# The first recurrence in a new order, with five masked levels of each leaf multiplied by TensorE one by one

## The chip, the cores and the metric

The kernel runs on one core of a Trainium2 chip. The metric is the device time of that core in microseconds (us), as a median of runs; lower is better. All tensors are float32. Five engines work from queues of their own, each strictly in the order in which its instructions were written: TensorE (PE, with its weight loads shown apart as PEld), VectorE (DVE), ScalarE (ACT), GpSimd (POOL) and SyncE (SP, which here only issues DMAs). They meet only at semaphores.

## The reference, cut to what matters

The program is two layers. Each is a modulated layer norm, a linear-attention recurrence with a residual, and a mixture of experts. The change touches the recurrence of the first layer alone (RWKV-6 on x of shape 2 x 1024 x 128, with two heads of 64; the 2 x 1024 tokens are handled as 8 chunks of 128 tokens of both batches).

```python
x_last = jnp.pad(x, ((0, 0), (1, 0), (0, 0)))[:, :t]      # x is the modulated norm
dxa = x_last - x
xm = x + dxa * miu_x
lora_h = jnp.tanh(xm @ A_lora).reshape(b, t, 5, -1)
miu = lambda_ + jnp.einsum('btfi,fic->fbtc', lora_h, B_lora)
xx = x[None] + dxa[None] * miu
w_in, k_in, v_in, r_in, g_in = xx
k = k_in @ Wk.T;  v = v_in @ Wv.T;  r = r_in @ Wr.T
g = jax.nn.silu(g_in @ Wg.T)
w = td_miu + jnp.tanh(w_in @ td_A) @ td_B
decay = jnp.exp(-jnp.exp(w))
# per head and token: S is 64 x 64, u a bonus for the token itself
def step(S, inp):
    ri, ki, vi, di = inp
    kv = ki[:, None] * vi[None, :]
    y = ri @ (S + uh[:, None] * kv)
    return di[:, None] * S + kv, y
# then a norm of y per head (eps 1e-5 * h), times g, times Wo.T, gate and residual
```

## The kernel before, in words

`rwkv_phase` (from L329) takes the 8 chunks one after another. `steps` (L480) writes them out: `front()` prepares chunk 0, then `step(i, q, prepare, tail)` runs for i = 0 to 7, and a last part normalises chunk 7. Buffers of a chunk's inputs have two copies, picked by q. In each call of `step`, every engine does three things mixed in an order fixed by hand:

- **the recurrence of chunk i.** Seven levels (m = 0 to 6) build, by doubling, the decayed r and k in the tiles rl[1..7], kl[1..7] and the products of decays tot[1..7]. At each level DVE multiplies tot and half of rl (L595, L596), POOL multiplies half of kl (L686), and ACT copies the other halves (L765, L767); every engine waits for the others at every level. PE multiplies k and r of a level within leaves of 32 tokens (`leaf_scores`, L855, slots 0 to 4 of the PSUM tile `pair`; slot 0 has the bonus) and, after level 5, the wider blocks (L913, L919). DVE masks the five slots (L613, into prod), adds them up (L616, into leafs) and copies the sum into the diagonal blocks of att (L621). ACT copies the blocks off the diagonal (L784 to L786). PE then multiplies rl[7] by state and att by v (L938, L941), and the transposed kl[7] (ktm, L929 and L776) by v (L946). DVE makes the new state from that (L626, L630).
- **the preparation of chunk i + 1** (prepare): norm (L504, DVE), transpose (L799), modulation (L713, ACT), difference (L641, POOL), lora_input (L510, DVE), two products (L804, L805), tanh (L718, L720, ACT), five small products (L814, L817), mix (L518 on DVE, then L646 on POOL, five instructions on each), and the projections to decay, k, v, r, g (L822 to L838) with their evacuations on ACT (L724 to L742). The last of them (eg, L742) tells that the chunk is ready.
- **the end of chunk i - 1** (tail): the norm of y per head (statistics L535 and L539, deviation L655 and L657 on POOL, normalise L544), transpose, scale, gate (L662), product with Wo (L873), gate and residual (L550, L667), and the input of the expert layer (moe_input, L558 to L572, with L673 and L675 on POOL).

What couples one step to the next is `start`, which DVE, POOL, ACT and PE pass at the head of a step:

```python
if not isinstance(i, int) or i:
    eng.wait_ge(s_state, i * 3)
eng.wait_ge(s_gT, i + 1)
```

So no engine begins the levels of chunk i before the state of chunk i - 1 is written. `keep_busy` (L865) puts 128 x 256 products whose result nobody reads into PE's queue, nine of them in a step with a tail and a preparation. Ahead of the levels, in each step, DVE also makes the four bonus tiles rd and kd (L584 to L587).

Of the kernel before, what the change touches and what calls it, by code (L numbers as in the profile page):

```python
# [22 lines left out]
P = 128  # L23
# [10 lines left out]
LEAF = 32  # L34
# [294 lines left out]
def rwkv_phase(nc, t, const, x_bc, eps_pow, mod_col, mod_row, bank, pair, cst, W0T, s_w0, mv, rstd, W1, s_w1, s_w2, sbw,  # L329
# [8 lines left out]
    with ExitStack() as ctx:  # L338
# [25 lines left out]
        rd = sb("rd", [P, N])  # L364
        kd = sb("kd", [P, N])
        vs = [sb(f"v_sb{q}", [P, BATCH, C]) for q in range(2)]
        eg = sb("eg", [P, N])
        gT = sb("gT", [P, N])
        prod = sb("prod", [P, 4, 160])
        leafs = sb("leafs", [P, 4, LEAF])  # L370
# [11 lines left out]
        s_zero = sem("s_zero")  # L382
        s_xn = sem("s_xn")
# [21 lines left out]
        s_leaf = sem("s_leaf")  # L405
        s_att = sem("s_att")
# [86 lines left out]
        def _(dve):  # L493
# [3 lines left out]
            dve.memset(hT[:, :, P:P + 1], 0.0).then_inc(s_zero, 1)  # L497
            dve.wait_ge(s_zero, 3)

            def norm(n):  # L500

                dve.tensor_copy(hT[:, :, 0:1], hT[:, :, P:P + 1]).then_inc(s_xn, 1)
                for b in range(BATCH):
                    dve.tensor_scalar(xn[:, b, :], x_bc[:, b, bass.ds(n, 1), :],  # L504
                                      mv[:, bass.ds(n + b * CHUNKS, 1), 0:1], rstd[:, bass.ds(n + b * CHUNKS, 1)],
                                      ALU.subtract, ALU.mult).then_inc(s_xn, 1)
# [14 lines left out]
            def gate(n):  # L521

                dve.scalar_tensor_tensor(out=gT[:, :], in0=eg[:, :], scalar=1.0, in1=bank[0][:, N:2 * N], op0=ALU.add,
                                         op1=ALU.mult).then_inc(s_gate, 1)

            def front():
                norm(0)
                lora_input(0)
                mix(0)
# [3 lines left out]
            def statistics(n, q):  # L533
                for u in range(4):
                    dve.bn_stats(gst[:, u, :], y[:, u, :]).then_inc(s_gn, 1)  # L535
# [18 lines left out]
            def moe_input(n, q):  # L554
# [9 lines left out]
                for b in range(BATCH):  # L564
                    dve.scalar_tensor_tensor(out=h_bc[:, b, bass.ds(n, 1), :], in0=x_bc[:, b, bass.ds(n, 1), :],
                                             scalar=nmv[:, b, 0:1], in1=sbw[:, 1, b:b + 1, :], op0=ALU.subtract,
                                             op1=ALU.mult).then_inc(s_nmod, 1)
                dve.wait_ge(s_nrstd, n * 2 + 2)
# [6 lines left out]
            def step(i, q, prepare, tail):  # L575
                rl, kl, tot = rls[q], kls[q], tots[q]
                start(dve, i)
                if prepare:
                    norm(i + 1)
                if tail:  # L580
                    statistics(i - 1, 1 - q)

                rh, kh = halves(rl[0], 0), halves(kl[0], 0)
                dve.tensor_scalar(halves(rd, 0)[:, :, 0], rh[:, :, 0], bonus[:, 0:1], None, ALU.mult).then_inc(s_diag, 1)  # L584
                dve.tensor_copy(halves(rd, 0)[:, :, 1], rh[:, :, 1]).then_inc(s_diag, 1)
                dve.tensor_copy(halves(kd, 0)[:, :, 0], kh[:, :, 0]).then_inc(s_diag, 1)
                dve.tensor_scalar(halves(kd, 0)[:, :, 1], kh[:, :, 1], bonus[:, 0:1], None, ALU.mult).then_inc(s_diag, 1)  # L587

                for m in lv:
                    if m:  # L590
                        dve.wait_ge(s_tot, i * LEVELS + m)
                        dve.wait_ge(s_r, i * LEVELS + m)
                        dve.wait_ge(s_rc, i * 2 * LEVELS + 2 * m)
                    tp = per(tot[m], m)
# [3 lines left out]
                    if tail and m == 0:  # L598
                        normalise(i - 1, 1 - q)
# [15 lines left out]
                dve.wait_ge(s_prod, i + 1)  # L615
# [1782 lines left out]
```

## Time and profile before

| | |
|---|---|
| median of 3 runs | 767.53 us (767.01 to 770.05) |
| the profiled execution | 770.7 us, its span 768.6 us |
| busy of the span | PE 86%, DVE 56%, ACT 38%, POOL 36% |
| mean granted TensorE clock | 0.931 |
| step 0 of the recurrence starts | 40.04 us after the start of the span |
| state of chunk 7 is written | 192.11 us |

The span is the time from the first to the last instruction; 2.1 us of the execution lie around it.
### The profile page before, as it was taken

The page shows a single profiled execution, that of the slowest core. Times are in us where ns is not written, and L with a number is a line of the kernel's source. Part 1 is how long each engine was busy: PE and PEld are TensorE (multiplying, and loading weights), DVE is VectorE, ACT ScalarE, POOL GpSimd, SP SyncE. Part 2 cuts the span into 40 slices and gives each one's busy share as a digit, 9 for nine tenths or more (in the row PEclk, how much of TensorE's full clock was granted, in tenths as well). Part 3 has the DMA queues.
Part 4 walks back from the last instruction along what each step waited for, and adds up shares of the span by engine and source line. Part 5 has one row for each costly group of instructions (what it writes and reads, how often), then busy time and mean ns, then how long its engine had stood idle before and what let it go on. Part 6 is the DMA issues. An engine that isn't in the chain of part 4 may idle for free.

```text
span 768.6 us, 26385 instructions
## 1 busy us (share of the span) xinstructions
PE 664.5 (86%) x10885; PEld 558.9 (73%) x10885; DVE 432.5 (56%) x1364; ACT 290.5 (38%) x964; POOL 277.2 (36%) x418
## 2 busy tenths in 40 slices
PE   4688888889721979699999999999999799999996
PEld 4356666657611968478888888888887599898996
DVE  4357888886250322265867776776767455344443
ACT  0154444442110422145555454454544235333321
POOL 1235555553234456100324233342423243222216
PEclk9769999989955989599999999999999899999999
DMA  6691000000214573200000000000040247575553
GB/s 176 215 275 27 3 1 3 3 2 2 110 42 152 165 236 119 58 3 4 3 10 12 11 11 14 11 11 14 7 144 10 80 149 253 182 246 197 186 211 90
DMA packets 45910, 66.31 MB, mean 86 GB/s; under 512 B 5584, under 2 KB 34736, under 8 KB 42848
## 3 DMA queue, kind: packets, MB, share of 16 engines
q1 hardware_dynamic: 42368, 57.55, 24.1%
q0 software_dynamic: 3424, 7.08, 2.6%
q8 instruction: 87, 1.43, 0.7%
q14 instruction: 31, 0.25, 0.1%
HBM read 49.92 MB, written 19.02 MB: 90 GB/s over the span
## 4 chain that ended last, share of the span: by engine, by line
PE 53%; DVE 2%; DMA 1%; issue 1%; another core or an unknown queue 1%; ACT 0%; SPq 0%; POOL 0%; DVEq 0%; POOLq 0%
PE bank L1720 6%; PE quad L1578 5%; PE quad L1702 5%; PE quad L1704 5%; PE bank L1603 4%; PE pair L1540 3%; PE bank L1627 3%; PE bank L1640 2%; PE quad L1584 2%; PE pair L1542 2%; PE pair L1541 2%; PE bank L1643 2%; PE bank L1630 2%; PE pair L1565 2%; DMA f_xg<-moe_slots 1%
## 5 line engine op out<-in xcount | busy, mean ns | idle before, releaser
L1978 DVE TENSOR_TENSOR h_masked<-quad,const 128x1536 f32<-128x1536 f32 (+2 forms) x66 | 112.5, 1704 | 55.1 <-PE quad L1584 45.5
L1814 ACT ACTIVATE f_sa<-quad 128x256 f32<-128x256 f32 (+1 forms) x115 | 40.2, 352 | 94.9 <-PE quad L1704 77.1
L2092 DVE TENSOR_TENSOR f_hid<-f_sa,quad 128x256 f32<-128x256 f32 (+1 forms) x115 | 43.0, 380 | 55.2 <-ACT f_sa L1814 54.8
L1702 PE MATMUL quad<-f_xT,f_w 128*128 128x256 f32 (+1 forms) x190 | 51.4, 353 | 3.6 <-DVE f_hid L2092 3.6
L1720 PE MATMUL bank<-f_w,f_hid 128*128 128x128 f32 x390 | 50.7, 277 | 1.1 <-DVE f_hid L2095 0.9
L1720 PEld LDWEIGHTS bank<-f_w,f_hid 128*128 128x128 f32 x390 | 47.8, 192 | 3.6 <-DVE f_hid L2095 2.8
L1704 PE MATMUL quad<-f_xT,f_w 128*128 128x256 f32 (+1 forms) x190 | 50.2, 346 | 0.0
L2201 POOL DMA_INDIRECT moe_slots<-g_pay,g_slot x28 | 28.7, 1023 | 58.3 <-DVE g_pay L1946 43.2
L1578 PE MATMUL quad<-h_qk 32*128 32x128 f32 x1024 | 47.1, 298 | 0.0
L868 PE MATMUL bank<-const 128*128 128x256 f32 x140 | 37.3, 406 | 7.8 <-PEq L202 7.8
L1603 PE MATMUL bank<-h_qk,h_state 32*32 32x128 f32 x1024 | 42.5, 274 | 0.0
L1578 PEld LDWEIGHTS quad<-h_qk 32*128 32x128 f32 x1024 | 34.8, 187 | 10.3 <-issue 8.4
L1791 ACT ACTIVATE h_gT<-bank 128x128 f32<-128x128 f32 x64 | 17.8, 278 | 64.9 <-PE bank L1630 64.9
L1103 POOL DMA_INDIRECT moe_out<-e_yg,e_token x32 | 30.9, 965 | 28.5 <-DVE e_yg L1203 22.2
L2167 POOL TENSOR_TENSOR h_added<-h_added,mod_row 128x128 f32<-128x128 f32 x16 | 7.3, 455 | 93.8 <-ACT h_added L1787 93.8
L2269 POOL DMA_INDIRECT moe_out<-f_y,f_token x31 | 30.3, 977 | 28.9 <-DVE f_y L2104 20.4
L686 POOL TENSOR_TENSOR kl<-kl,tot 128x128 f32<-128x128 f32 x56 | 25.2, 449 | 40.6 <-DVE state L630 20.8
L1765 ACT ACTIVATE h_qk<-pair 128x256 f32<-128x256 f32 x64 | 24.5, 383 | 36.8 <-PE pair L1542 36.8
L1702 PEld LDWEIGHTS quad<-f_xT,f_w 128*128 128x128 f32 x190 | 32.3, 195 | 6.7 <-DVE f_hid L2092 3.9
L1704 PEld LDWEIGHTS quad<-f_xT,f_w 128*128 128x128 f32 x190 | 34.2, 195 | 3.4
L868 PEld LDWEIGHTS bank<-const 128*128 128x128 f32 x140 | 26.6, 203 | 11.4 <-issue 8.0
L1795 ACT ACTIVATE h_oT<-bank 128x128 f32<-128x128 f32 x64 | 17.8, 278 | 40.7 <-PE bank L1652 32.2
(380 smaller groups left out, 1840.0 us busy)
## 6 DMA issues: line engine op xcount, KB each, us to landing
f_w<-moe_w SPq DMA_DIRECT2D x23, 1088.0 KB, 5.2
e_w<-in_experts_dram SPq DMA_DIRECT2D x32, 257.5 KB
moe_slots<-blank SPq DMA_DIRECT2D x2, 2112.0 KB, 16.6
moe_slots<-zero SPq DMA_DIRECT2D x4, 516.0 KB, 4.0
e_xg<-moe_slots SPq DMA_DIRECT2D x8, 258.0 KB
f_xg<-moe_slots SPq DMA_DIRECT2D x12, 132.0 KB, 4.5
moe_w<-in_moe_w_dram SPq DMA_DIRECT2D x1, 1408.0 KB, 7.5
moe_w<-in_moe_w_dram SPq DMA_DIRECT2D x1, 1280.0 KB, 10.5
```

The costliest lines, as they stand in the source:

```text
L868: pe.matmul(bank[of][:, 0:N], cst("ident"), const[:, 0:N], start=True, stop=True)
L1103: pool.indirect_dma_start(out=t["moe0_out"], out_offset=bass.IndirectOffsetOnAxis(ap=token_of[s][:, k:k + 1], axis=0), in_=yg[s][:, k, :], ...
L1578: last = pe.matmul(quad[:, h, a * P:(a + 1) * P], qk[q][head(h), 1 - a, :], qk[q][head(h), a, :], start=True, stop=True, tile_position=(h ...
L1603: pe.matmul(left[head(h), part * P:(part + 1) * P], states[k][head(h), (0 if part else 2 * D):(D if part else 3 * D)], qk[k][head(h), 1 - ...
L1702: pe.matmul(up_bank(n, f)[:, 0:s], w[:, F1 + TAIL1 + f * P:F1 + TAIL1 + (f + 1) * P], x_of(n)[:, 0:s], start=True, stop=True)
L1704: pe.matmul(up_bank(n, f)[:, T1:T1 + s], w[:, f * P:(f + 1) * P], x_of(n)[:, 0:s], start=True, stop=True).then_inc(f_up, 1)
L1720: pe.matmul(acc[k], hid[n % 2][:, f, cols], w[:, 2 * F1 + f * C:2 * F1 + (f + 1) * C], start=(f == 0), stop=False)
L1814: act.activation(sa[g % 3][:, 0:s], up_bank(n, f)[:, 0:s], ACT.Silu).then_inc(f_sa, 1)
L1978: dve.tensor_tensor(masked[k % 4][:, :, a * P:z * P], quad[:, :, a * P:z * P], cst("causal")[:, None, a * P:z * P].to_broadcast([P, HPG, ( ...
L2092: dve.tensor_tensor(hid[n % 2][:, f, 0:s], sa[g % 3][:, 0:s], up_bank(n, f)[:, T1:T1 + s], ALU.mult)\
L2201: pool.indirect_dma_start(out=t["moe1_slots"], out_offset=bass.IndirectOffsetOnAxis(ap=slot[:, b * 2 + k:b * 2 + k + 1], axis=0), in_=pay[ ...
L2269: pool.indirect_dma_start(out=t["moe1_out"], out_offset=bass.IndirectOffsetOnAxis(ap=token_of[n % 2][:, k:k + 1], axis=0), in_=yg[n % 2][: ...
```

## The change

1. **Start of a step.** `start` waits for the leaf products of the step before (s_leafmm) in place of its state. State, kv and the statistics of y of chunk i - 1 move into step i, behind level 2 on DVE (`carry`). Level 6 on DVE waits for s_kv of the step before, and level 6 on POOL and ACT for its transposed keys (s_ktT), since the tiles would be overwritten.
2. **The leaf.** L616 and L621 go, and with them the tile leafs. After the mask, PE multiplies each of the 5 masked levels, each of the 4 leaves and each head and batch by v on its own: 80 products of 32 x 32 by 32 x 64, placed on the diagonal tiles of the array, all added into the same PSUM bank between rl[7] x state and att x v.
3. **Bonus tiles and norm go to ACT.** rd and kd have two copies and are written by ACT straight from PSUM, four activations more; the norm of x (`centre`) is two activations, one and a half steps ahead, and its transpose stands at the end of a step, for chunk i + 2.
4. **Order.** difference behind level 0; DVE's mix behind level 4; POOL's mix behind level 5; on PE the mix products after slot 3, and the projections, all of them, before L913 and L919; `take_decay_r_g` on ACT before the copies into att, and ktm last in ACT's step; the expert input of chunk i - 2 in step i, in two pieces; gate at the head of a step, gT with two copies.
5. **keep_busy.** Two products in a step with tail and preparation in place of nine.

```diff
@@ start
-            if not isinstance(i, int) or i:
-                eng.wait_ge(s_state, i * 3)
+            if i:
+                eng.wait_ge(s_leafmm, i)
             eng.wait_ge(s_gT, i + 1)
@@ VectorE, step
-                if prepare:
-                    norm(i + 1)
-                if tail:
-                    statistics(i - 1, 1 - q)
...
+                    last_column(i + 1)
+                gate(i, q)
                 for m in lv:
...
+                    if i and m == LEVELS - 1:
+                        dve.wait_ge(s_kv, i)
...
+                    if m == 2:
+                        if i >= 2:
+                            moe_statistics(i - 2)
+                        if tail:
+                            statistics(i - 1, 1 - q)
+                            carry(i - 1, 1 - q)
                     if m == 4:
+                        if prepare:
+                            mix(i + 1)
+                        if i >= 2:
+                            moe_scale(i - 2)
                         if tail:
-                            dve.wait_ge(s_zg, i)
-                        gate(i)
-                        if tail:
-                            output(i - 1, 1 - q)
-                if prepare:
-                    mix(i + 1)
+                            normalise(i - 1, 1 - q)
...
                                   cst("leaf")[:, None, :].to_broadcast([P, 4, 160]), ALU.mult).then_inc(s_prod, 1)
-                dve.wait_ge(s_prod, i + 1)
-                dve.tensor_reduce(leafs[:, :, :], prod[:, :, :].rearrange("p u (l n) -> p u n l", n=LEAF), AX.X,
-                                  ALU.add).then_inc(s_leaf, 1)
...
-                    dve.tensor_copy(att[rows, :, rows], leafs[rows, :, :]).then_inc(s_att, 1)
                 if tail:
-                    moe_input(i - 1, 1 - q)
...
+                    output(i - 1, 1 - q)
@@ GpSimd, step
-                    if prepare and m == 1:
+                    if prepare and m == 0:
                         difference(i + 1)
...
+                    if m == 2:
+                        if i >= 2:
+                            moe_deviation(i - 2, q)
+                        if tail:
+                            deviation(i - 1, 1 - q)
+                    if prepare and m == 5:
+                        mix(i + 1)
                 if tail:
+                    gated_heads(i - 1, 1 - q)
                     add(i - 1, 1 - q)
@@ ScalarE, take_k_v, take_decay_r_g, step
+                act.activation(kd[:, :, 0], k0[:, :, 0], ACT.Copy).then_inc(s_evac, 1)
+                act.activation(kd[:, :, 1], k0[:, :, 1], ACT.Copy, scale=bonus[:, 0:1]).then_inc(s_evac, 1)
...
+                act.activation(rd[:, :, 0], r0[:, :, 0], ACT.Copy, scale=bonus[:, 0:1]).then_inc(s_diag, 1)
+                act.activation(rd[:, :, 1], r0[:, :, 1], ACT.Copy).then_inc(s_diag, 1)
...
+                    if prepare and m == 2:
                         lora_tanh(i + 1)
...
+                    if m == 3 and i + 2 < CHUNKS:
+                        centre(i + 2)
+                    if m == 5:
+                        if i:
+                            act.wait_ge(s_kv, i)
+                        if prepare:
+                            decay_tanh(i + 1)
+                            take_k_v(i + 1, 1 - q)
+                        if tail:
+                            scale_heads(i - 1, 1 - q)
                 if prepare:
+                    take_decay_r_g(i + 1, 1 - q)
...
-                act.wait_ge(s_leaf, i + 1)
+                act.wait_ge(s_prod, i + 1)
                 act.activation(att[0:64, :, 64:128], scores[0:64, :, 160:224], ACT.Copy).then_inc(s_off, 1)
...
                 if prepare:
+                    act.wait_ge(s_ktT, i + 1)
+                    act.activation(ktm[:, :, :], bank[4][:, 0:N].rearrange("p (b n) -> p b n", b=BATCH),
+                                   ACT.Copy).then_inc(s_ktm, 1)
@@ TensorE, step
-                keep_busy(5 if tail else 2)
+                keep_busy(2)
                 start(pe, i)
-                if prepare:
-                    transpose_x(i + 1)
-                if tail:
-                    keep_busy(2)
...
+                if prepare:
+                    project_k_v(i + 1)
+                if tail:
+                    transpose_heads(i - 1, 1 - q)
+                if prepare:
+                    project_decay_r_g(i + 1)
+                else:
+                    keep_busy(5, 2)
...
                 last.then_inc(s_leafmm, 1)
+                if tail:
+                    output(i - 1, 1 - q)
+                if i + 2 < CHUNKS:
+                    transpose_x(i + 2)
...
+                pe.wait_ge(s_prod, i + 1)
                 for b in range(BATCH):
                     pe.matmul(bank[5][:, b * P:(b + 1) * P], rl[7][:, b * P:(b + 1) * P], state[:, b, :],
                               start=True, stop=False, skip_group_check=True)
+                    for l in range(5):
+                        for h in range(RW_HEADS):
+                            for k in range(4):
+                                rows = slice(k * LEAF, (k + 1) * LEAF)
+                                pe.matmul(bank[5][rows, b * P + h * RW_DIM:b * P + (h + 1) * RW_DIM],
+                                          prod[rows, h * BATCH + b, l * LEAF:(l + 1) * LEAF],
+                                          v_sb[rows, b, h * RW_DIM:(h + 1) * RW_DIM], start=False, stop=False,
+                                          tile_position=(k * LEAF, k * LEAF), skip_group_check=True)
+                    if b == 0:
+                        pe.wait_ge(s_off, i * 3 + 3)
                     for h in range(RW_HEADS):
...
+                if prepare:
+                    pe.wait_ge(s_k, i * LEVELS + 7)
...
+                    for b in range(BATCH):
+                        last = pe.transpose(bank[4][:, b * P:(b + 1) * P], kl[7][:, b * P:(b + 1) * P], cst("ident"))
+                    last.then_inc(s_ktT, 1)
+                    pe.wait_ge(s_ktm, i + 1)
```

## Rows read from the trace of the kernel before

**Rows 1.** Windows, one for each step: length, busy of each engine, PEclk, DMA share.
```profile
core 0: us, PE busy (x) PEld busy (x) DVE busy (x) ACT busy (x) POOL busy (x), PEclk, DMA share, GB/s
40.04:59.81 19.77, 17.65 (x241) 12.30 (x241) 11.81 (x37) 8.81 (x29) 6.69 (x13) 0.72 1.16 262
...
97.48:116.25 18.77, 16.04 (x258) 11.23 (x257) 15.75 (x58) 9.16 (x30) 10.89 (x19) 1.00 0.00 1
...
154.31:175.69 21.38, 18.32 (x253) 13.23 (x253) 15.83 (x59) 9.37 (x30) 10.89 (x19) 0.84 0.01 2
175.69:192.11 16.42, 14.64 (x248) 11.63 (x247) 12.14 (x50) 5.24 (x19) 7.34 (x13) 1.00 0.01 2
```

**Rows 2.** Timeline of step 3, from its start to the mix.
```profile
97.51 0.32 ACT L765 ACTIVATE rl<-rl 128x128 f32<-128x128 f32 x1 [2.34 <-DVE state L630]
...
98.34 0.61 DVE L535 BATCH_NORM_STATS2 gst<-bank 128x6 f32<-128x64 f32 x4
...
99.01 0.81 ACT L713 ACTIVATE hT<-quad,mod_col 128x128 f32<-128x128 f32 x2 [0.97 <-PE quad L799]
...
100.19 1.17 POOL L657 TENSOR_TENSOR grs<-grs,eps_pow 128x4 f32<-128x4 f32 x1
...
101.76 0.61 POOL L641 TENSOR_TENSOR dxa<-hT 128x256 f32<-128x256 f32 x1
...
102.75 0.67 DVE L510 SCALAR_TENSOR_TENSOR xm<-dxa,miu,hT 128x256 f32<-128x256 f32 x1
...
106.99 0.33 PE L913 MATMUL pair<-rl,kl 64*32 64x32 f32 x16
...
107.41 2.04 DVE L518 SCALAR_TENSOR_TENSOR xx<-quad,lamb,dxa 128x256 f32<-128x256 f32 x5
107.63 0.44 PE L929 MATMUL bank<-const,kl 128*128 128x128 f32 x2
108.03 3.01 POOL L646 TENSOR_TENSOR xx<-xx,hT 128x256 f32<-128x256 f32 x5
108.11 0.39 ACT L776 ACTIVATE ktm<-bank 128x256 f32<-128x256 f32 x1 [0.77 <-PE bank L929]
```

**Rows 3.** The same timeline, from the mask to the next start.
```profile
109.37 0.81 DVE L613 TENSOR_TENSOR prod<-pair,const 128x640 f32<-128x640 f32 x1
...
109.90 0.30 PEld L826 LDWEIGHTS quad<-xx,wT 128*128 128x128 f32 x2 [0.99 <-POOL xx L646]
...
110.98 0.70 PE L832 MATMUL quad<-tw,td_b 64*128 64x256 f32 x2
...
112.14 0.59 PE L838 MATMUL quad<-xx,wT 128*128 128x256 f32 x2
...
112.50 0.49 DVE L558 BATCH_NORM_STATS2 nst<-x_sb 128x6 f32<-128x128 f32 x2
...
112.59 0.46 PE L938 MATMUL bank<-state,rl 128*128 128x128 f32 x2
...
112.88 0.56 PE L941 MATMUL bank<-v_sb,att 128*128 128x64 f32 x4
...
113.28 0.44 PE L938 MATMUL bank<-state,rl 128*128 128x128 f32 x2
113.38 0.62 DVE L565 SCALAR_TENSOR_TENSOR h_pay<-x_sb,nmv,sbw 128x128 f32<-128x128 f32 x2
...
116.28 0.33 ACT L765 ACTIVATE rl<-rl 128x128 f32<-128x128 f32 x1 [2.35 <-DVE state L630]
```

**Rows 4.** Timeline of PE in the second layer: products on 32 x 32 tiles.
```profile
402.39 0.29 PE L1603 MATMUL bank<-h_qk,h_state 32*32 32x128 f32 x4
...
402.50 0.29 PE L1603 MATMUL bank<-h_qk,h_state 32*32 32x128 f32 x4
```

**Rows 5.** Windows within step 6, before and in its stretch at the lower clock.
```profile
163.50:167.10 3.60, 2.41 (x32) 1.26 (x31) 3.47 (x10) 1.30 (x5) 3.40 (x6) 1.00 0.02 5
167.10:173.90 6.80, 6.80 (x24) 5.48 (x23) 4.04 (x13) 2.99 (x9) 1.80 (x4) 0.50 0.00 0
```

More of the change, by code:

```diff
@@ L614, in step, with last_norms @@
                                   cst("leaf")[:, None, :].to_broadcast([P, 4, 160]), ALU.mult).then_inc(s_prod, 1)
[L615 to L633 removed]
+                if tail:
+                    output(i - 1, 1 - q)
+            def last_norms(n, q):
+                moe_statistics(n - 1)
+                normalise(n, q)
+                moe_scale(n - 1)
+                output(n, q)
+                moe_statistics(n)
+                moe_scale(n)
+            steps(dve, front, step, (statistics, last_norms))
         @block.gpsimd
@@ L707, in _, with centre @@
             act.wait_ge(s_w0, LOADS)
+            def centre(n):
+                for b in range(BATCH):
+                    c = n + b * CHUNKS
+                    act.activation(xn[:, b, :], x_bc[:, b, n, :], ACT.Identity, bias=nbias[:, c:c + 1],
+                                   scale=rstd[:, c:c + 1]).then_inc(s_xn, 1)
             def modulate(n):
                 act.wait_ge(s_xt, n + 1)
-                act.wait_ge(s_xn, n * 3 + 1)
+                act.wait_ge(s_last, n + 1)
                 for b in range(BATCH):
@@ L846, in front @@
                 mix(0)
[L847 removed]
+                project_k_v(0)
+                project_decay_r_g(0)
+                transpose_x(1)
             def leaf_scores(slot, k_op, r_op):
@@ L939, in step @@
                               start=True, stop=False, skip_group_check=True)
-                    for h in range(RW_HEADS):
-                        pe.matmul(bank[5][:, b * P + h * RW_DIM:b * P + (h + 1) * RW_DIM], att[:, h * BATCH + b, :],
-                                  v_sb[:, b, h * RW_DIM:(h + 1) * RW_DIM], start=False, stop=True,
-                                  skip_group_check=True)
-                pe.wait_ge(s_ktm, i + 1)
-                for b in range(BATCH):
-                    last = pe.matmul(bank[5][:, N + b * P:N + (b + 1) * P], ktm[:, b, :], v_sb[:, b, :], start=True,
-                                     stop=True, skip_group_check=True)
+                    for l in range(5):
[6 more added lines that the diff above has]
+                                          tile_position=(k * LEAF, k * LEAF), skip_group_check=True)
@@ new lines, in step @@
+                    if b == 0:
+                        pe.wait_ge(s_off, i * 3 + 3)
+                    for h in range(RW_HEADS):
+                        last = pe.matmul(bank[5][:, b * P + h * RW_DIM:b * P + (h + 1) * RW_DIM],
+                                         att[:, h * BATCH + b, :], v_sb[:, b, h * RW_DIM:(h + 1) * RW_DIM],
+                                         start=False, stop=True, skip_group_check=True)
+                if prepare:
+                    pe.wait_ge(s_k, i * LEVELS + 7)
+                    if tail:
+                        pe.wait_ge(s_gated, i)
+                    for b in range(BATCH):
+                        last = pe.transpose(bank[4][:, b * P:(b + 1) * P], kl[7][:, b * P:(b + 1) * P], cst("ident"))
+                    last.then_inc(s_ktT, 1)
+                    pe.wait_ge(s_ktm, i + 1)
+                    for b in range(BATCH):
+                        last = pe.matmul(bank[5][:, N + b * P:N + (b + 1) * P], ktm[:, b, :], v_sb[:, b, :], start=True,
+                                         stop=True, skip_group_check=True)
```

137 lines of the change are left out of this document (57 added, 80 removed).

## The prediction

> **What bounds the kernel now.** I went first to the windows, one for each step of the recurrence [rows 1]. Step 0 takes 19.77 us, steps 1 to 5 together the 94.50 us from 59.81 to 154.31, so 18.90 each, step 6 takes 21.38 and step 7, which prepares nothing, 16.42. PE is busy for 16.0 of 18.8 us in step 3, but nine of its products in each step only keep it awake, DVE is busy for 15.8, ACT for 9.2, POOL for 10.9: no engine is full, so a step is a chain of waits. I then followed that chain in the timeline of step 3 [rows 2, 3]. It starts at 97.51, when ACT and POOL have waited for the last write of state. It runs by ACT's modulation (99.01), the difference on POOL (101.76), lora_input on DVE (102.75), the levels, DVE's mix (107.41) and POOL's mix (108.03): 10.5 us after the start. From there two strands run side by side: the projections on PE (109.90 to 112.73), and the mask (109.37), the sum and the copies on DVE, until PE's L938 begins at 112.59. Then come att x v, kv and the state, and step 4 starts at 116.28. So I cut a step into head (start to POOL's mix, 10.5), middle (mix to mask, 1.3) and end (mask to next start, 6.9), 18.8 in all.
>
> **What starts a step after the change.** DVE and POOL may start once the leaf products of the step before are done, but each of them does one level alone: level 1 needs ACT's copies of level 0. ACT writes ktm last in its step, ktm needs the transposes on PE, and those stand in PE's queue behind all products with prod and att. So the true start of a step is still one point, ACT behind ktm, and the waits at the head of the other engines are hidden under it. From here time 0 is that point, and the clock is first taken as full.
>
> **The head.** ACT's two copies of level 0 and the two modulations: 0.5 + 0.81 = 1.3, since the transpose was made a step earlier (before it came 1.5 us into the step) [rows 2]. The difference on POOL, now ahead of level 1, 0.61 and its handoff: 2.0. lora_input 0.67: 2.7. Level 2 on DVE: 0.3, to 3.0. Behind it stand three blocks. The expert statistics of chunk i - 2 take from 112.50 to the end of L565 at 114.00, 1.5 us [rows 3]: 4.5. Statistics of y and deviation, up to the power on POOL, took from 98.34 to 101.36, 3.0 us [rows 2]: 7.5. POOL can make level 3 only then (0.45), ACT copies level 4 (0.55), POOL makes level 5 (0.4): mix at 8.9. The carry on DVE (kv 0.42, state 0.61) lies beside the power and costs nothing, nor do the two tanh and the products for them (ready by 6), nor DVE's mix, which begins at about 7.3; if POOL's power were not there, DVE's mix would set POOL's start to 7.9. The head gains 10.5 - 8.9 = 1.6 us.
>
> **The middle.** Before, the leaf products L913 and L919 were through (107.7) before the mix had begun on POOL, and the mask waited only for DVE's own mix. Now they stand behind all projections. From POOL's mix to the k product 1.87 (108.03 to 109.90), k and v 1.08 (to 110.98), two transposes of the heads 0.25, the three products of decay, r and g 1.75 (110.98 to 112.73), the leaf products 0.7 (106.99 to 107.63, and their drain): 5.7 us [rows 2, 3]. The middle loses 5.7 - 1.3 = 4.4 us. This is the term that decides.
>
> **The end.** Mask 0.81. The sum over levels and the copies go (109.37 + 0.81 to 112.59, 2.4 us with the handoff). In their place stand the 80 products. No row shows such a series with 64 columns, so I bound it. Groups of four 32 x 32 products with 128 columns follow each other on the same tiles after 0.11 us (402.39, 402.50), all four at once and into one bank [rows 4]. A group's record is half a product, so a whole product of 128 columns costs 0.22, of 64 columns 0.11 if the columns set the pace. Twenty groups in a row on the same tiles make 2.2 us. From below: if a product's second record cost nothing beside its first, half of that, 1.1. From above: if every record took the full 0.11 at 64 columns too, 4.4. I take 2.2, since columns set the pace in the row that is nearest. To it comes 0.1 for each of the two changes to the small tiles. rl[7] x state and att x v took 0.69 for a batch (112.59 to 113.28) [rows 3], so PE needs 2 x (0.69 + 1.1 + 0.1) = 3.8. The copies of ACT off the diagonal end at about the time at which PE is through with the first batch's small products; they are hidden, with almost nothing to spare. Then the transposes of kl[7], 0.48 until ACT can read them (107.63 to 108.11), and ktm 0.3 to 0.4 [rows 2]. Sum 0.85 + 3.8 + 0.5 + 0.35 = 5.5, against 6.9: the end gains 1.4. In between, output(i - 1) and transpose_x fill PE while it waits for the mask; four more activations on ACT (about 1.2 us) and scale_heads, level 6 and the two decays put eg at about 16 and the copies into att at 16.6, just as late as PE wants them.
>
> **Sum at full clock.** 8.9 + 5.7 + 5.5 = 20.1, say 20.0, against 18.9: 1.1 us slower for each of the steps 2 to 6. Step 1 has no expert statistics yet, so its head is 1.5 shorter: 18.5. Step 0 has neither those nor a chunk to normalise; its head shrinks by about 1 and its middle grows like the others', so I count +2 with the low clock that it has anyway. Step 7 together with the closing norms has the shorter start and drops kv: -1. The front gets four activations, two of them ahead of eg: +0.5.
>
> **The clock.** Step 6 shows what a lower clock costs [rows 5]. There PE was busy for only 2.41 of the 3.6 us before 167.10, and then the granted clock was 0.50, 1.2 GHz, for 6.8 us in which the projections and the output products lay. The step took 21.38, 2.5 us more than the average of 1 to 5. Steps 1 to 5 hold the same work and kept their clock, so the kernel before stands near the edge. After the change the same stretch is much emptier. In my times PE makes the mix products until about 6, slot 4 (0.4) at 8, the td product (0.65) at 9.5 and the k product at 10.8: about 1.1 us busy in 4.8, and seven of nine keep_busy are gone. I therefore expect one stretch at 1.2 GHz in every step, just behind that gap, where the chain now runs through PE only, for 2.5 us each as in step 6. The ends are 0, if the clock holds, and 5, if it stays low until the next gap.
>
> On the clock, the Trainium skill (TensorE: Matmul & The Clock Gate, Part 1) says that the half rate is the default state and that only sustained activity of PE lifts it. The trace agrees as far as [rows 5] go. By that rule the removal of keep_busy counts against this change, which is what I have.
>
> **Forecast.** Step 1: 18.5 + 2.5 - 18.9 = +2.1. Steps 2 to 5: (20.0 + 2.5 - 18.9) x 4 = +14.4. Step 6: 22.5 - 21.4 = +1.1. With +2 for step 0, +0.5 for the front and -1 at the close: +19.1. From the profiled 770.7 that gives 789.8. That execution stands 3.2 above the median of 767.5, and the low stretch of step 6 explains 2.5 of it if the typical run has none. The changed kernel would have it in either case, so its median lies where its profile does, less the 0.7 that is left: 789. I say 788, because a stretch can miss a step.
>
> **Rivals.**
> - *The clock holds.* Then only the order counts: against a median run without a low stretch, -0.4 for step 1, +1.1 x 5, +1.5 at both ends: +6.6, about 774; with errors of half a us for a step, 770 to 778. For it: in steps 1 to 5 the clock held over PE's gaps. Against it: none of those gaps is as long.
> - *Faster: the head is far shorter.* The chain through POOL's power and level 3 is my own reading of the handwritten order. If the three blocks on DVE found their inputs so early that POOL's mix began at 6.9, a step would take 18.0 at full clock and not leave so large a gap for the clock. Place: DVE between level 2 and 4; price -0.9 x 6 and -1 at the close: 761. It decides from a head under 7.8. For it: all inputs of these blocks are a step old. Against it: DVE has 1.5 + 1.0 + 1.0 of instructions there by its own durations.
> - *The small products don't run at once.* If the four tiles of a group waited for each other, 80 x 0.11 = 8.8 instead of 2.2: +6.6 for 8 steps, about 840. Against it [rows 4], where four products of the same kind into one bank start within one 0.11 us.
>
> The Trainium skill (TensorEngine Tiling (Array Packing), Gotcha 1) states that different row tiles can't access the same PSUM bank simultaneously. All four leaves write one bank from four row tiles. By that rule the last rival would hold, with its 840; [rows 4] disagree, and the measured spacing decides.
>
> **Chances.** Forecast 0.57, between 779 and 799; clock holds 0.20; faster 0.16; small products serial 0.03; the rest, a mixture with two low stretches or another stall, 0.04, above 800. A measurement of this kernel tells 0.5% from no change, 3.8 us: under 763.7 is faster, over 771.4 slower. Faster: 0.14. Same: the nearest edges of the second and third case, 0.11. Slower: 0.75. The range reaches down to 765, into the faster case's upper edge, and up to 802, which is nearly a second stretch (2.3 us more) in each of six steps.
>
> **What would show it.** The steps, from one L765 of level 0 to the next, last 22 to 23 us, with PEclk near 0.84. POOL's L646 begins about 9 us after the start, and the mask 5.7 us behind it, more at the low clock. ACT's first copy of a step waits for PE's transposes and ktm, not for DVE. The 80 products take 1.1 us for a batch. I am wrong if ACT begins a step before PE has ended the last, if the small products take 4 us or more, or if PEclk is 1.00 in the steps.

## The result and the profile after

| | before | after |
|---|---|---|
| median | 768.76 us (767.01 to 770.05, 4 runs) | 798.89 us (795.10 to 801.34, 4 runs) |
| ratio | | 1.0389, 95% interval 1.0333 to 1.0445 |
| profiled execution, span | 770.7, 768.6 | 795.1, 793.3 |
| mean granted clock | 0.931 | 0.901 |
| last write of h_pay, end of the stage | 202.49 | 232.57 |

The change is slower by 30.1 us, with 19.1 worked out and 788 forecast. The profiled execution of the kernel before (770.7) is slower than each of the runs behind its median, and that of the changed kernel (795.1) is the fastest of its four, so the two profiles differ by only 24.4 us. The windows of the changed kernel, one for each of four steps and the close (columns as in [rows 1]):

```profile
core 0: us, PE busy (x) PEld busy (x) DVE busy (x) ACT busy (x) POOL busy (x), PEclk, DMA share, GB/s
39.86:62.37 22.51, 19.46 (x392) 13.38 (x391) 8.31 (x27) 10.02 (x36) 7.29 (x14) 0.72 0.99 223
62.37:84.64 22.27, 19.67 (x402) 13.96 (x402) 10.81 (x39) 10.54 (x37) 9.57 (x17) 0.77 0.01 3
108.46:132.27 23.81, 19.68 (x402) 13.93 (x402) 12.91 (x47) 10.54 (x37) 10.74 (x19) 0.78 0.01 2
180.32:205.51 25.19, 21.00 (x400) 15.06 (x400) 12.90 (x46) 9.78 (x36) 10.73 (x19) 0.73 0.01 3
205.51:232.57 27.06, 24.36 (x438) 19.58 (x438) 14.80 (x66) 5.40 (x20) 11.18 (x20) 1.00 0.01 2
```

Steps 1 to 6 took 115.88 us (59.84 to 175.72) and now take 143.14 (62.37 to 205.51). In [rows 1] the clock was 1.00 in every step but 0 and 6. Now it is below 0.80 in all of them, with one stretch at 1.2 GHz in each, 10.2 us long in steps 0 to 5 and 13.7 in step 6. PE is busy for 19.7 of 23.8 us, though it has seven keep_busy products less; much of that is the same work at half the pace. Here are the lines of step 3 in the timeline of the changed kernel that answer to [rows 2, 3]:

```profile
108.18 0.38 ACT L820 ACTIVATE ktm<-bank 128x256 f32<-128x256 f32 x1 [4.49 <-PE bank L996]
108.46 0.31 ACT L792 ACTIVATE rl<-rl 128x128 f32<-128x128 f32 x1
...
109.10 0.22 DVE L600 TENSOR_TENSOR tot<-tot 128x64 f32<-128x64 f32 x1 [4.05 <-ACT kl L794]
...
109.75 0.61 POOL L642 TENSOR_TENSOR dxa<-hT 128x256 f32<-128x256 f32 x1 [4.85 <-ACT hT L729]
...
114.48 1.12 POOL L658 TENSOR_TENSOR grs<-grs,eps_pow 128x4 f32<-128x4 f32 x1
...
116.08 0.39 PE L894 MATMUL pair<-rl,kl 64*32 64x32 f32 x32 [1.70 <-POOL kl L689]
...
117.10 3.28 POOL L647 TENSOR_TENSOR xx<-xx,hT 128x256 f32<-128x256 f32 x5
117.80 1.11 PE L857 MATMUL quad<-xx,td_a 128*64 128x256 f32 x2 [1.32 <-POOL xx L647]
...
119.13 1.22 PE L861 MATMUL quad<-xx,wT 128*128 128x256 f32 x2 [0.22 <-POOL xx L647]
...
121.56 1.22 PE L869 MATMUL quad<-tw,td_b 64*128 64x256 f32 x2
...
124.71 0.44 PE L955 MATMUL pair<-rl,kl 64*32 64x32 f32 x16
...
125.82 0.82 DVE L621 TENSOR_TENSOR prod<-pair,const 128x640 f32<-128x640 f32 x1 [5.22 <-PE pair L961]
...
127.71 1.32 PE L981 MATMUL bank<-v_sb,prod 32*32 32x64 f32 x80
```

The step starts where I had put it: ACT has waited 4.49 us for PE's transposes, then makes ktm, then level 0, and DVE has waited 4.05 for that. The head is 8.64 us (108.46 to 117.10). The middle is 8.72 (117.10 to 125.82), since it lies in the low stretch: the product of decay (L869), for one, now needs 1.22 us where it took 0.70. The end is 6.45 (125.82 to the next start at 132.27). In the windows, the gap ahead of the low stretch (which began at 117.5) and the stretch itself are these:

```profile
114.40:117.80 3.40, 0.39 (x33) 0.31 (x33) 3.31 (x12) 1.10 (x5) 2.97 (x6) 0.96 0.02 5
117.50:127.70 10.20, 9.68 (x48) 6.46 (x48) 4.58 (x16) 5.07 (x17) 4.32 (x8) 0.50 0.01 2
```

In the gap PE did 0.39 us of work in 3.40, against 2.41 in 3.60 ahead of the low stretch of [rows 5].

### The profile page after: what moved, and what is told of

Read it like the earlier page. It is cut to its first block, busy times and chain, and to the rows that moved or that the text cites. A ratio compares the mean times of both kernels' runs of the same rounds, so it can differ in the third digit from the quotient of the medians.

```text
span 793.3 us, 28739 instructions
## 1 busy us (share of the span) xinstructions
PE 684.6 (86%) x12067; PEld 574.3 (72%) x12067; DVE 407.4 (51%) x1274; ACT 301.0 (38%) x1011; POOL 276.0 (35%) x418
## 4 chain that ended last, share of the span: by engine, by line
PE 52%; DVE 2%; issue 1%; another core or an unknown queue 1%; DMA 1%; ACT 0%; POOL 0%; SPq 0%; DVEq 0%; POOLq 0%
PE bank L1774 6%; PE quad L1632 5%; PE quad L1756 5%; PE quad L1758 5%; PE bank L1657 4%; PE pair L1594 3%; PE bank L1681 3%; PE bank L1694 2%; PE quad L1638 2%; PE pair L1595 2%; PE pair L1596 2%; PE bank L1684 2%; PE bank L1697 2%; PE pair L1619 2%; PE bank L1776 1%; PE quad L1761 1%
## 5 line engine op out<-in xcount | busy, mean ns | idle before, releaser
L1845 ACT ACTIVATE h_gT<-bank 128x128 f32<-128x128 f32 x64 | 17.8, 278 | 64.5 <-PE bank L1684 64.5
L1632 PEld LDWEIGHTS quad<-h_qk 32*128 32x128 f32 x1024 | 34.7, 187 | 10.2 <-issue 8.0
L600 DVE TENSOR_TENSOR tot<-tot 128x128 f32<-128x128 f32 (+6 forms) x56 | 17.0, 303 | 36.1 <-ACT kl L794 34.4
L1849 ACT ACTIVATE h_oT<-bank 128x128 f32<-128x128 f32 x64 | 17.8, 278 | 42.0 <-PE bank L1706 32.5
L1594 PE MATMUL pair<-h_hT,hla_wq 128*128 128x128 f32 x128 | 30.7, 323 | 2.5 <-POOL h_hT L2215 1.8
```

Source lines behind the costliest of these rows:

```text
L1594: pe.matmul(proj[:, 0:P], W["q"][:, cols], hT[b][:, :], start=True, stop=True)
L1632: last = pe.matmul(quad[:, h, a * P:(a + 1) * P], qk[q][head(h), 1 - a, :], qk[q][head(h), a, :], start=True, stop=True, tile_position=(h ...
```

## Experiments

The chips differ: the kernel before had medians of 747.3 (e1, e2, e4, e5), 746.5 (e3, e6 to e8), 765.2 (e9, e10) and 746.0 us (e11, e12). So I compare ratios to it, the times of steps, and the end of the stage (the last write of h_pay), which lies in the first third of the program. Step 0 starts anywhere between 38.0 and 40.1 us in these profiles, so the end of the stage is good to some 2 us. Head, middle and end are those of the prediction: start to POOL's mix, mix to mask, mask to the next start.

| run | ratio (95%) | end of stage | a full-clock step: head + middle + end |
|---|---|---|---|
| e1_filled_gap | 1.0176 (1.0102 to 1.0249) | 213.3 | 8.64 + 5.76 + 5.92 = 20.32 |
| e2_same_fill_early | 1.0504 (1.0424 to 1.0584) | 241.5 | none at full clock |
| e4_before_less_fill | 1.0425 (1.0348 to 1.0502) | 227.1 | none at full clock |
| e5_before_80_products | 1.0297 (1.0225 to 1.0369) | 225.2 | 10.51 + 1.34 + 9.19 = 21.04 |
| e3_filled_dve_sum | 1.0173 (1.0115 to 1.0231) | 210.1 | none at full clock (20.04 at 0.92) |
| e7_early_keys | 1.0299 (1.0226 to 1.0371) | 211.4 | 10.14 + 5.89 + 2.03 = 18.06 |
| e6_early_keys_filled | 0.9982 (0.9945 to 1.0019) | 198.3 | 10.14 + 5.90 + 2.03 = 18.07 |
| e8_early_keys_dve_sum | 0.9926 (0.9893 to 0.9959) | 193.7 | about 17.8 |
| e9_leaf_before_decay | 1.0205 (1.0144 to 1.0265) | 209.3 | 8.64 + 4.07 + 7.17 = 19.88 |
| e10_more_fill | 0.9950 (0.9925 to 0.9975) | 202.0 | 9.85 + 5.91 + 2.03 = 17.79 |
| e11_fill_att_wait | 0.9867 (0.9825 to 0.9908) | 189.5 | 9.98 + 5.76 + 2.14 = 17.88 |
| e12_e8_again | 0.9932 (0.9897 to 0.9967) | 192.4 | 9.85 + 5.91 + 2.03 = 17.79 |

### Clock or order

e1_filled_gap, in the changed kernel:

```diff
                             mix(i + 1)
+                            keep_busy(4)
...
                 if prepare:
+                    keep_busy(3)
                     project_k_v(i + 1)
```

> The changed kernel with seven 128 x 256 keep_busy products more in each step that prepares a chunk, four behind the mix products and three behind slot 4, into the stretch in which PE is nearly idle. My theory (the loss is one stretch at 1.2 GHz in each step, caused by that gap, on top of an order that is slower by about 1.1 us for a step): PEclk 1.00 in the steps, a step of 20.0 us in place of 23.8, time about 776 to 779. Rival (the clock is only a companion; PE's serial work at any clock sets the step, and the filler costs what it gives): a step stays at 23 to 24 us, time 795 to 800.

Two of its windows:

```profile
82.72:103.04 20.32, 18.86 (x416) 13.70 (x416) 12.86 (x47) 10.17 (x38) 10.67 (x19) 1.00 0.01 3
144.45:164.77 20.32, 18.84 (x416) 13.67 (x416) 12.86 (x47) 10.17 (x38) 10.67 (x19) 1.00 0.01 3
```

PEclk is 1.00 and a step takes 20.32 us (20.0 expected; steps 3 and 6, with a longer end at full clock, took 21.1 and 20.9). Idle products that nobody reads make a step 3.5 us shorter. So the 4.9 us by which a step of 23.8 stands over the old 18.9 split into 3.5 for the clock and 1.4 for the order. Over steps 1 to 6 together, 8.1 us of the change's 27.3 remain in e1 (123.96 us against 115.88) and 19.2 are gone. On its chip the kernel stays 1.8% slower than before (0.9 to 1.3% expected), and its stage ends 10.8 us later than in the profile of before.

e2_same_fill_early puts the same seven products where the kernel before has them:

```diff
                 start(pe, i)
+                keep_busy(5)
...
                     if m == 1:
+                        keep_busy(2)
```

> The changed kernel with the same seven keep_busy products more, but at the places where the kernel before has them: five at the head of a step, two behind slot 1. My theory (the place counts: the gap between the mix products and the projections stays as it is): PEclk 0.77 to 0.79 in the steps, a step of 23.8 to 24.5, time 797 to 803. Rival (the number of idle products per step counts): as with the filled gap, PEclk near 1.00, time 776 to 779.

A low stretch stayed in every step, 6.8 to 10.2 us long in steps 1 to 5, which took 24.1 to 25.5 us, and 3.4 us long in step 6, which took 22.3. The ratio got no better. Two windows of it: PEclk is 0.79 and 0.86.

```profile
90.93:115.60 24.67, 22.48 (x416) 16.59 (x416) 13.03 (x47) 10.43 (x38) 10.47 (x19) 0.79 0.01 2
140.08:164.13 24.05, 21.40 (x416) 15.81 (x416) 13.04 (x47) 10.41 (x37) 10.47 (x19) 0.86 0.01 3
```

With the same seven products, the place of the idle work decides here; the head was 9.67, a whole us longer than with the fill in the gap.

e4_before_less_fill is the kernel before with `keep_busy(2)` for `keep_busy(5 if tail else 2)` and without the two pairs behind `transpose_x` and slot 1.

> The kernel before with two keep_busy products in a step in place of nine, all else unchanged. If the old order's gaps are short enough by themselves, as my theory has it, the clock falls in some steps and not in all: 768 to 780, 2.5 us for each step that has a low stretch. If the number of idle products is what holds the clock (rival), every step 1 to 6 has a low stretch: about 784 or more.

Here I missed. One of its steps:

```profile
151.02:174.93 23.91, 19.79 (x242) 13.23 (x242) 15.53 (x59) 9.36 (x31) 10.92 (x19) 0.64 0.01 2
```

The clock stood at 0.50 for 17.1 us of each of steps 2 to 6, these steps took 23.9 to 24.1 us, and the ratio is 1.0425: as much as the whole loss of the change, with nothing else of it in. So the seven products ahead of level 2 are what holds the clock in the old order. Its low stretch began at 155.8, and in the 3.40 us ahead of that PE had done 0.86 us of work. That gap lies in the head, where the seven products had stood. So this run does not part the number of idle products from their place: in both orders they held the clock where they filled the stretch that was empty without them, and in the old order that stretch is another one (e2 shows that filling it does not help the new order).

### What the 80 products cost

e5_before_80_products, in the kernel before, has L616 and L621 out and this in:

```diff
-                pe.wait_ge(s_att, i * 4 + 4)
-                pe.wait_ge(s_off, i * 3 + 3)
+                pe.wait_ge(s_prod, i + 1)
...
+                    for l in range(5):
+                        for h in range(RW_HEADS):
+                            for k in range(4):
+                                rows = slice(k * LEAF, (k + 1) * LEAF)
+                                pe.matmul(bank[5][rows, ...], prod[rows, ...], v_sb[rows, ...], ...)
+                    if b == 0:
+                        pe.wait_ge(s_off, i * 3 + 3)
```

> The kernel before with one part of the change alone: no sum over levels (L616) and no copies (L621) on DVE, the 80 small products on PE in their place. My theory: PE is busy with the projections until 112.7 in step 3 anyway, when att was ready at 112.5, so what DVE saves gives nothing and the 80 products add their 2.5 us to each of 8 steps: 768.8 + 20 = about 788. Rival (the sum on DVE, 1.26 + 0.96 us, was on the path, and the products replace it one for one): 768 to 773.

From its timeline, step 2:

```profile
95.74 0.81 DVE L612 TENSOR_TENSOR prod<-pair,const 128x640 f32<-128x640 f32 x1
...
98.51 0.59 PE L830 MATMUL quad<-xx,wT 128*128 128x256 f32 x2
...
98.94 0.38 PE L929 MATMUL bank<-state,rl 128*128 128x128 f32 x2
99.26 1.32 PE L935 MATMUL bank<-v_sb,prod 32*32 32x64 f32 x80
...
100.51 0.66 PE L942 MATMUL bank<-v_sb,att 128*128 128x64 f32 x4
```

Forty products (80 records) take 1.25 us (99.26 to 100.51): their records start over 1.10 us, and the next product 0.15 behind the last of them, close to the 1.1 and 0.1 that I had. PE takes up rl[7] x state only at 98.94, behind the projections, 2.4 us after the mask is ready, so DVE's saving is worth nothing. The end grows from 6.9 to 9.19, by 2.3 us. The run is 21 us slower than before on its chip (20 expected), but that this agrees so well is partly luck: 2.3 us in eight steps are 18, and in the profile steps 3 and 4 took 24.2 us with a low stretch of 6.8 us in each, and step 6 took 22.4 with one of 3.4.

e3_filled_dve_sum goes the other way: e1_filled_gap with the old reduction and copies put back, and PE's wait for s_att in place of the small products.

> The changed kernel with the filled gap of e1_filled_gap and with the old sum on DVE (reduction and four copies) in place of the 80 products. Theory (each costs about its own duration at the end of a step: 2.3 us of products on PE, as the kernel before with the products alone showed, against 1.26 + 0.96 us on DVE, of which PE's output, transposes and waits for ACT hide little): the end of a step about 5.4 us against 5.9, head and middle unchanged, total 2 to 4 us less than e1_filled_gap. Rival (the products run beside other work in the new order and are free, the DVE sum is not): the end grows to 7 to 8 us, total 7 to 14 more.

```profile
114.66 0.82 DVE L624 TENSOR_TENSOR prod<-pair,const 128x640 f32<-128x640 f32 x1 [2.81 <-PE pair L973]
...
115.51 1.24 DVE L627 TENSOR_REDUCE leafs<-prod 128x128 f32<-128x640 f32 x1
...
116.79 0.97 DVE L632 COPY att<-leafs 32x128 f32<-32x128 f32 x4
...
117.90 0.63 PE L993 MATMUL bank<-v_sb,att 128*128 128x64 f32 x4 [1.82 <-DVE att L632]
...
119.74 0.31 ACT L802 ACTIVATE rl<-rl 128x128 f32<-128x128 f32 x1
```

The end is 5.08 (114.66 to 119.74) against 5.92. Hence in the new order too the products cost 0.8 us a step more than the sum they replace. PE now idles for 1.82 us there, and low stretches of 3.4 to 6.8 us came back (0.83 and 0.92 in two windows). They lie about the start of a step; PE is then late with the idle products, so the td product begins 10.65 us into the step and not 9.60 as in e1, and the middle is 6.3. The theory is right on the term. The total is open: the stage ends 3.2 us sooner than in e1, and the ratio, the same as that of e1, has an interval of 4 us to either side.

### Is the middle the term that decides?

e9_leaf_before_decay: e1_filled_gap with the leaf products ahead of `project_decay_r_g`.

> The changed kernel with the filled gap of e1_filled_gap, and the leaf products L913 and L919 ahead of the projections of decay, r and g on PE. My prediction called the middle (mix to mask, 5.7 us) the term that decides. If PE's serial work sets the step (theory, as the traces of the changed kernel now show it), the middle shrinks by 1.7 us to about 4.0, the end grows by as much to about 7.6, and a step stays at 20.3 us: total within 3 us of e1_filled_gap. If the late mask itself holds the step up (rival), the end stays at 5.9 and a step takes 18.6: 10 to 12 us less than e1_filled_gap.

```profile
151.57 3.28 POOL L647 TENSOR_TENSOR xx<-xx,hT 128x256 f32<-128x256 f32 x5
...
155.64 0.82 DVE L621 TENSOR_TENSOR prod<-pair,const 128x640 f32<-128x640 f32 x1 [0.56 <-PE pair L959]
...
162.81 0.31 ACT L792 ACTIVATE rl<-rl 128x128 f32<-128x128 f32 x1
```

The mask begins 1.7 us sooner (4.07 behind POOL's mix), and the end grows by 1.25 (7.17 against 5.92). A step gains 0.4 and not 1.7, and the ratio (1.0205) is not below that of e1 (1.0176). So the place of the leaf products is not what costs; what costs is that PE goes through projections, leaf products, output and small products one behind another, and only then makes the transposes for which the next step waits.

### Taking the transposes out of that row

e7_early_keys is the changed kernel with one block moved:

```diff
+                if prepare:
+                    pe.wait_ge(s_k, i * LEVELS + 7)
+                    if tail:
+                        pe.wait_ge(s_gated, i)
+                    for b in range(BATCH):
+                        last = pe.transpose(bank[4][:, b * P:(b + 1) * P], kl[7][:, b * P:(b + 1) * P], cst("ident"))
+                    last.then_inc(s_ktT, 1)
                 if i:
                     pe.wait_ge(s_state, i * 3)
                 pe.wait_ge(s_prod, i + 1)
```

(the same lines are taken out behind the output products). e6_early_keys_filled adds `keep_busy(2)` behind the mix products and `keep_busy(1)` ahead of `project_k_v`.

> The changed kernel with one move: PE transposes kl[7] before the output products and not behind them, no idle product added. Theory (what starts a step is ACT behind ktm, and ktm waits in PE's queue behind the output products): the end shrinks from 5.9 us at full clock to about 2.6, the head grows by about 1 since PE is busy with the old step's products when the new one wants its lora products, and a step takes about 18 us if the clock holds in the now shorter gap, 21 if it falls: 6 us less than the kernel before, or 12 to 15 more. Rival (a step starts when DVE and POOL are free, or the work lost at the end comes back at the head in full): step as in the changed kernel, 23 to 24 us, and 25 to 30 more than the kernel before.

> The same move, with three keep_busy products in each step for the gap, two behind the mix products and one behind slot 4. Theory: PEclk 1.00, a step of 18 to 18.5 us, total about 4 to 8 us less than the kernel before. Rival (end given back at the head): a step of 20.3 as in e1_filled_gap, 12 us more than the kernel before.

Step 3 of e6_early_keys_filled in its timeline:

```profile
96.19 1.32 PE L990 MATMUL bank<-v_sb,prod 32*32 32x64 f32 x80
96.35 0.31 ACT L792 ACTIVATE rl<-rl 128x128 f32<-128x128 f32 x1
...
98.30 1.32 PE L990 MATMUL bank<-v_sb,prod 32*32 32x64 f32 x80
...
106.49 3.11 POOL L647 TENSOR_TENSOR xx<-xx,hT 128x256 f32<-128x256 f32 x5
...
112.39 0.82 DVE L621 TENSOR_TENSOR prod<-pair,const 128x640 f32<-128x640 f32 x1 [2.07 <-PE pair L963]
...
114.42 0.31 ACT L792 ACTIVATE rl<-rl 128x128 f32<-128x128 f32 x1
```

ACT starts the new step (96.35) while PE is still at the old one's products. The end falls from 5.92 to 2.03, the head grows by 1.5, and a step takes 18.07 us in place of 20.32. Both runs agree on that; what separates them is the clock: e7 has steps of 18.06 beside steps of 21.4, with 1.00 and 0.83 in the windows. Its total missed both expectations: 18.9 us more than the kernel before, where I had 12 to 15 with the clock fallen; step 1 alone took 25.82. With the fill the kernel is level with the one before (0.9982, its interval holds 1). I had expected 4 to 8 us less: step 1 took 23.55, of which 3.26 us are a stall that I come to at the end (e7 has one of 3.14).

e8_early_keys_dve_sum puts the sum on DVE there as well, with `output(i - 1, 1 - q)` between mask and reduction.

> The same move and fill, with the old sum on DVE in place of the 80 products, DVE's output for the chunk before standing ahead of the reduction. Theory: now DVE's 2.2 us stand before its first level of the next step, which ACT could start 2.6 us behind the mask: DVE is free only 3.5 us behind it, so the end grows by about 1, while PE is free 2.3 earlier for the head's lora products, which gives about 1 back: the same as e6_early_keys_filled within 3 us. Rival (the products cost 2.3 us in any order): 10 to 15 us less than e6_early_keys_filled.

It is 5.2 us below e6_early_keys_filled (739.35 and 744.51 on one chip), between the two expectations. Its full-clock steps are 0.3 shorter; the bulk is step 1 (18.26 against 23.55), where the stall among the 80 products is gone with them. The last three runs keep to it:

> The kernel e8_early_keys_dve_sum (early transposes of the keys, DVE's sum) with five idle products in the gap in place of three. Its trace still had four stretches at the lower clock between 100 and 185 us, and two of its steps took 20.0 and 18.8 in place of 17.8. Theory (the clock is what is left): no low stretch there, all steps 17.8 to 18.2, total 2 to 4 us less than e8_early_keys_dve_sum. Rival (two more products of 0.46 us stand before the td product and lengthen the head): steps of 18.3 to 18.8, total the same or 3 us more.

The rival was nearer: five idle products in the gap in place of three left seven low stretches in the profile and did not beat e8 (0.9950 and 0.9926, intervals overlapping, on different chips). That profile is the slowest of its ten runs, 4.1 us above their median, so it may show more low stretches than most.

e11_fill_att_wait adds one line behind the early transposes, `keep_busy(3, 5)`, where PE waited 1.55 us for att; e12_e8_again is e8 unchanged.

> The kernel e8_early_keys_dve_sum with three idle products more, at another place: behind the early transposes, where PE waited 1.55 us for att. In e10_more_fill two more in the first gap had not raised the clock. Theory (the stretch that lets the clock fall is this wait together with the time around it, not the gap behind the mix): PEclk 1.00 in the steps, all of them 17.8 to 18.0, total 3 to 6 us less than e8_early_keys_dve_sum on the same chip. Rival (the low stretches come from elsewhere, and the products only make PE later): the same or up to 3 us more.

> The kernel e8_early_keys_dve_sum once more, unchanged, for a comparison on one chip with e11_fill_att_wait and for its own ratio to the kernel before. Theory (the gain is real): again 0.5 to 1.1% less than the kernel before. Rival (the first result hung on how the low stretches fell): within 0.3% of it.

Two windows of e11_fill_att_wait:

```profile
88.63:106.51 17.88, 15.60 (x256) 11.04 (x255) 14.41 (x53) 10.30 (x38) 10.93 (x20) 1.00 0.01 2
142.18:159.97 17.79, 15.36 (x254) 10.66 (x253) 14.28 (x53) 9.60 (x35) 10.43 (x20) 1.00 0.02 4
```

All its steps 2 to 6 take 17.8 to 17.9 us at full clock; e12 had steps of 18.4 to 18.6 beside such ones, each with a low stretch of 3.4 us that began behind the wait for att (in the 3.40 us ahead of the one at 91.9 PE had done 1.85 us of work). On one chip their medians are 734.13 and 739.68, 5.5 us apart, and e12 came out at 0.9932, within what I had expected of e8 (0.5 to 1.1% less). In the profiles the stage differs by 2.9 us; that of e12 is the fastest of its twelve runs. e11 is the best version: 0.9867 of the kernel before, 11.9 us less (745.99), so it beats that one clearly, and the changed kernel (1.0389) by the ratios. What it keeps of the change is the start of a step, the order, and the work moved to ACT; which of these carries the gain, no run has parted. What it drops are the 80 products.

## Why the prediction was right, and where not

- **The time**: 798.89 is 10.9 us above the 788 and 0.1 below the upper edge of the range that the forecast named, 779 to 799. That it fell inside is partly luck: the stage lost 11 us more than I had summed, the rest of the program gave 5.4 back, and the median came 3.8 above the profiled execution, where I had put it 0.7 below.
- **What starts a step** (ACT behind ktm): right, in the chain lines above and in e6, where the step starts sooner once ktm does.
- **Head** 8.9: measured 8.64 at either clock, by the strands I named. Right.
- **Middle** 5.7: 5.76 at full clock (e1), 8.72 with the low stretch in it. The size was right. My sentence that this term decides was wrong: e9 took 1.7 us out of it and the step kept all but 0.4. It was a part of one serial row on PE.
- **End** 5.5: 5.92. The 80 products cost 2.3 to 2.5 a step, as estimated, and output(i - 1) and transpose_x are hidden under the mask at full clock, as I had it (in e1 PE still waits 0.16 us for the mask). What I had too short are the products about them: a batch took 2.12 us (98.09 to 102.33 in e1 for two), where I had 1.9. At 1.2 GHz the two blocks stick out behind the mask, and the end is 6.45.
- **Order at full clock** 20.0: 20.32.
- **The clock**: the mechanism was right (e1 against e2). Its size is the term that I mis-sized, *"for 2.5 us each as in step 6"*: the low stretches were 10.2 us long where that of [rows 5] was 6.8, and cost 3.5 each (23.8 - 20.3). Hence steps of 23.8 and a clock of 0.79, where I had named 22 to 23 and 0.84. The steps of e7 show the price by length: 20.80 us with a stretch of 6.8, 21.44 with one of 10.2, 18.06 with none. I also wrote that the chain runs through PE only there, which should have told me that it costs more than in the old order, where POOL and DVE set part of the pace.
- **The sum**: steps 1 to 6 +27.3 (17.6 forecast), step 0 +2.7 (+2), front -0.2 (+0.5), close +0.3 (-1): the stage +30.1 against +19.1. (That the medians differ by the same 30.1 is chance.) The close did not gain: from its mask on it is 1.7 us shorter, but the mask came 11.16 us after the start of step 7 where it was 9.13. Five idle products stand ahead of the leaf products there (213.66 to 215.91); in e9, where they stand behind, the mask came after 9.00.
- Behind the stage the profiled span gave 5.4 us back (566.1 to 560.7 us from the last h_pay to the end). The code there is the same in all runs, and on chips of like speed this rest was 569.3 in e9 and 562.1 in e10. It goes with the granted clock of that rest: 0.93 before and 0.95 after, 0.93 in e9 and 0.94 in e10, and on one chip 549.2 us at 0.94 (e7) and 541.6 at 0.95 (e6). What moves the clock there, no run has tried.
- **Rivals.** *The clock holds*, for which I gave about 774, is e1: +11.6 on its chip, where I had +6.6. *The head is far shorter*: no run shows it; where the inputs wait for PE (e6) it is longer. Its 761 also left out the +2 of step 0 and the +0.5 of the front that the other sums have; with them it is 763.6. *The small products don't run at once*: refuted by the 1.25 us for 40 of them; four row tiles did write one bank side by side.

## What to carry to other kernels

Look for the one instruction behind which the next iteration starts, and for what stands ahead of it in the queue of the engine that feeds it: moving two transposes ahead of 4.2 us of products for which the next start need not wait took a step from 20.3 to 18.1 us, more than the 1.4 by which the order of the change had lengthened it. Work moved to the engine whose queue already is the serial row cost nearly its full duration here, however well it was packed (2.3 us a step in e5, for 2 x 1.25); DVE's 2.2 us were cheaper (e3, e8). And when an order is changed, the idle products that hold the clock have to be placed anew, from the new trace: first into its longest empty stretch (e1), then where the next low stretch begins (e11), since two more in the first place did nothing (e10).

## What I had not expected of the hardware

- Seven products of 0.46 us whose result nobody reads decide over 3.5 us a step in the new order (e1) and 5 in the old (18.9 to 23.9, e4). With only two of them the granted clock was 0.64 over a whole step of the old order.
- Products on 32 x 32 tiles start four abreast: in e5 the records of four tiles, with 64 columns each, start within 0.02 us, the next four 0.056 us later, into one PSUM bank, with a weight load each; 80 records take 1.25 us.
- A long series of small products can stall. In e6_early_keys_filled PE stopped inside the 80 records of a batch of chunk 0 and waited for nothing that the profile shows:

```profile
56.02 1.19 PE L990 MATMUL bank<-v_sb,prod 32*32 32x64 f32 x66
60.46 0.64 PE L990 MATMUL bank<-v_sb,prod 32*32 32x64 f32 x14 [3.26 <-issue]
```

  In the same batch it stopped for 2.71 us in e1, 3.14 in e7, 3.05 in e9 and 0.88 in e5, and not in the changed kernel or e2. The DMA engines were full until the stall began, mostly with copies of the expert weights, and idle when it ended (a share of 1.23 from 54.00 to 57.20, 0.41 from 57.20 to 60.46, 0.00 behind that). The changed kernel has 1182 more MATMUL records on PE (591 products) and fetched 96 packets of instructions on queue 8 where the one before had 87. That PE waited for its instructions behind those copies fits, but no run tried it, and it leaves open why two kernels with the 80 products did not stop.
